# Three-bank rings in PSUM, one TensorE semaphore per step, and a step's other matmuls in front of its sums, in a graph network kernel

## The chip, the core and the metric

The kernel runs on one core of a Trainium2 chip. The metric is device time in microseconds. Before, it was 2964.37 us (median of 3 runs, 2962.93 to 2966.32). The core's engines are TensorE (PE; its weight loads are shown as PEld), VectorE (DVE), ScalarE (ACT), GpSimd (POOL) and SyncE (SP). Each works through a queue of its own in order, and they wait for each other by semaphores.

## The reference

100,000 edges in order of their target run between 6250 nodes of 256 features; each edge has 32 attributes and one of three types. Three layers of

```python
ew = edge_attr @ edge_w + edge_b                 # the same in every layer
inv_cnt[i] = 1 / max(segment_sum(mask_i, dst), 1)
for l in range(3):
    msg = relu(x[src] * ew)
    out = sum_i (segment_sum(msg * mask_i, dst) * inv_cnt[i]) @ weights[l, i]
    out = out + x @ roots[l] + biases[l]
    x = x + relu(out)
return layernorm(x_in + x)
```

## The kernel before

**Tiles and steps.** The edges are 782 tiles of 128; a step q has two tiles, a layer NP = 391 steps. For each tile GpSimd gathers 128 rows of x from HBM (`gather`, L700: an indirect DMA of 128 KB into the ring `xg`, XR = 12 tiles). TensorE makes the edge weights of both tiles in PSUM (`edge_weights`, L867: turned attributes `at` against two parts of `edge_w`). DVE multiplies (L1300), ACT applies the ReLU (L791), TensorE sums by target and type against the 0/1 selectors `S` (`collect`, L911, 4 matmuls of 96 columns, each recorded in two parts), and DVE adds the 96-column result to `acc` in SBUF (`add_sums`, L1138). `S` is made by DVE every other step from a row of numbers kept in PSUM bank 5 (`selectors`, L1097).

**Blocks.** The nodes are NB = 49 blocks of 128, finished in the order `blocks` from step `starts[k]` on (14, 22, 34 ... 374, 393). For each: x is loaded and turned (`turn_x`, L936, bank 4, copied by ACT, L799), four products with the layer's matrices (`mix`, L961, one step each, banks 6 and 7), and DVE's five operations (`block_ops`, L1155 to L1194). SP stores the new rows to the next x and, shifted by one block, to a copy y, from which the next layer's first 12 gathers read while the last block is unfinished.

**Layer 0 alone** also turns the attributes: SP loads four tiles' attributes (`load_attr`), ACT rounds a copy (`high`, L745), DVE subtracts it (`split`, L1012, 128x128), TensorE transposes the four tiles into bank 4 (`attr_turn`, L846), and ACT copies them into `at` (`attr_copy`, L753); SP keeps `at` in HBM (`keep_attr`) and loads it again in layers 1 and 2. It also counts edges by target and type: two matmuls a step (L903), an addition (`add_counts`, L1251), and a matmul per block (`count`, L924).

**Order.** Every engine's queue is written out by hand, step by step. TensorE in iteration q: `edge_weights(q+1)`, `count`, `collect(q-1)`, `mix`, `attr_turn`, `turn_x`. DVE: product q, `add_sums(q-2, 0)`, `selectors`, `split`, block operations, counts, `add_sums(q-2, 1)`. PSUM banks 0 and 1 hold edge weights in turn, 2 and 3 the sums. TensorE has semaphores for the edge weights (`s_e`), each tile's sums (`s_sc`), transposes (`s_tr`, `s_xt`), counts (`s_cm`) and pairs of block products (`s_d0`, `s_d1`). A gather waits until the sums have read its ring slot: `eng.wait_ge(s_sc, 2 * ((n - XR) // 2 + 1))`.

Of the kernel before, what the change touches and what calls it, by code (L numbers as in the profile page):

```python
# [62 lines left out]
def gnn_program(nc, x_in, src, dst, edge_attr, edge_type, weights, roots, biases, edge_w, edge_b,  # L63
                src_t, dst_t, typ_t, head, head7, head4, due, out):
# [7 lines left out]
    NT = 782  # L72
# [10 lines left out]
    XR, SR, TR, AR = 12, 8, 3, 6  # L83
    XB, XT, TB = 4, 2, 4
    PAD = 1000000
    BR = 196
# [29 lines left out]
    with ctx:  # L116
# [18 lines left out]
        hs = sb("hs", [128, 3, 4, 64])  # L135
# [8 lines left out]
        cnt = sb("cnt", [128, 148])  # L144
        diff = sb("diff", [128, 128])
        brow = sb("brow", [128, BR], I32)
# [43 lines left out]
        def columns(k):  # L190
# [20 lines left out]
        s_an = sems("s_an", 3)  # L211
        s_hi, s_lo, s_tr, s_atc = sem("s_hi"), sem("s_lo"), sem("s_tr"), sem("s_atc")
# [3 lines left out]
            "s_oh", "s_ob", "s_cn", "s_cm", "s_inv", "s_df"))  # L216
        s_w = sem("s_w")
        s_xl = sems("s_xl", XB)
        s_x0 = sems("s_x0", 2)
        s_xt, s_xc, s_d0, s_d1, s_f0, s_f1, s_nm, s_z = (sem(n) for n in (  # L220
            "s_xt", "s_xc", "s_d0", "s_d1", "s_f0", "s_f1", "s_nm", "s_z"))
# [4 lines left out]
        s_dm, s_d2, s_hz = sem("s_dm"), sem("s_d2"), sem("s_hz")  # L226
# [22 lines left out]
        short = order.index(quad(NT - 1))  # L249

        def attrs(g):

            return 16 * (g // 3 + 1) + (16 if g % 3 == short % 3 and g >= short else 0)

# [19 lines left out]
        def products(k, m):  # L274

            b = pD[m // 2] if k < NB - 1 else (pT, pT, pD[0], pD[1])[m]
            return b[0:rows(k), 256 * (m % 2):256 * (m % 2) + 256]

        def sums_bank(l, q, i):

            V = l * NP + q
            return pA[(V + (i if q == NP - 1 else 0)) % 2]
# [5 lines left out]
        def twice(K, i):  # L288

            return sum(n % NB < NB - 1 for n in range(i, min(K, NB * (L - 1)), TB))  # L290

# [19 lines left out]
        end = starts[-1] + 16  # L311
# [20 lines left out]
        G_an = hs[:, 0, 0, 0:32]  # L332
# [139 lines left out]
        def general(eng, name):  # L472
# [31 lines left out]
            if name == "sync":  # L504
                eng.wait_ge(s_z0, 2)
                eng.wait_ge(s_src, 32)
                eng.wait_ge(s_pc, 9)
                eng.wait_ge(s_atc, 1)
                for i in range(XR):
                    eng.wait_ge(s_g[i], 16)  # L510
                for g in range(3):
                    eng.wait_ge(s_an[g], attrs(g))
# [31 lines left out]
        def _(eng):  # L544
# [10 lines left out]
            def load_attr(g):  # L555
                if g >= 3:
                    eng.wait_ge(s_tr, g - 2)
                a, n = 128 * head_tile(order[g]), tiles_of(g) - (g == short)
                if g == short:
                    eng.wait_ge(s_hz, 1)  # L560
                    eng.dma_start(hs[0:LAST, g % 3, 3, 32:64], edge_attr[128 * (NT - 1):E, :]).then_inc(s_an[g % 3], 16)
                eng.dma_start(hs[:, g % 3, 0:n, 32:64], edge_attr[a:a + 128 * n, :]
                              .rearrange("(j p) d -> p j d", p=128)).then_inc(s_an[g % 3], 16)

            def keep_attr(g):
                w = 128 * tiles_of(g)
                eng.wait_ge(s_atc, g + 1)
                eng.dma_start(attr_t[g, :, 0:w], at[0:64, g % TR, 0:w].bitcast(F32)).then_inc(s_ao[g % TR], 16)

            def reload_attr(l, g):  # L570
                G = l * NG + g
                eng.wait_ge(s_e, l * NP + 2 * max(0, g - TR + 1))
# [32 lines left out]
            load_attr(2)  # L605
            eng.dma_start(idx[:, 0:2], src_t[:, 0:2]).then_inc(s_src, 16)

            def load_sources(l):
                for k in hosts_k:
                    eng.wait_ge(s_d1, NB * l + k + 1)  # L610
# [6 lines left out]
            def fast():  # L617
                for l in range(L):
                    late = (13, 9, 15)[l]
                    for q in range(-4, end):  # L620
                        if l == 0 and q % 2 == 0:
                            if 3 <= q // 2 + 4 < NG:
# [33 lines left out]
                        for k in starting(q, 8 if l else 12):  # L656
                            if k + XB < NB:
                                load_x(l, k + XB)
                        for k in starting(q, 9):
# [11 lines left out]
        def _(eng):  # L671
            eng.memset(p_ew, 0.0).then_inc(s_ez, 1)
            eng.memset(zcol[:, :], 0.0).then_inc(s_zc, 1)
            eng.memset(hs[:, short % 3, 3, 32:64], 0.0).then_inc(s_hz, 1)
# [52 lines left out]
        def _(eng):  # L727
# [14 lines left out]
            def high(g):  # L742

                eng.wait_ge(s_an[g % 3], attrs(g))
                eng.activation(hs[:, g % 3, :, 0:32].bitcast(F32R), hs[:, g % 3, :, 32:64], ACT.Copy).then_inc(s_hi, 1)  # L745

            def attr_copy(g):
                w = 128 * tiles_of(g)
                eng.wait_ge(s_tr, g + 1)
                if g >= TR:  # L750
                    eng.wait_ge(s_e, 2 * (g - TR + 1))
                    eng.wait_ge(s_ao[g % TR], 16 * (g // TR))
                eng.activation(at[0:64, g % TR, 0:w], pT[0:64, 0:w], ACT.Copy).then_inc(s_atc, 1)  # L753
# [3 lines left out]
            attr_copy(0)  # L757
# [19 lines left out]
            def fast():  # L777
                for l in range(L):
                    for q in range(-6, end):
# [12 lines left out]
                        if l == 0 and q % 2 == 0 and 1 <= (q + 2) // 2 < NG:  # L792
                            attr_copy((q + 2) // 2)
                        for k in [k for k in range(NB) if q == turn_step(k) + 1]:
                            K, n = NB * l + k, rows(k)
                            eng.wait_ge(s_xt, K + 1)
                            if K >= XT:
                                eng.wait_ge(s_d0, K - XT + 1)
# [598 lines left out]
```

## Time and profile before

| | |
|---|---|
| median of 3 runs | 2964.37 us |
| the profiled execution's own span | 3581.6 us |
| busy PE / PEld | 2843.8 us (79%) / 2613.2 us (73%) |
| busy DVE | 2148.4 us (60%) |
| busy ACT | 1289.4 us (36%) |
| busy POOL | 2224.3 us (62%) |
| granted TensorE clock, mean | 0.896 |
| chain that ended last | PE 59%, issue 17%, DVE 9% |
| moved by DMA | 465.42 MB in 334989 packets |

Busy times are of the one recorded execution; shares are of its span. Matmuls are pipelined and their ends are modelled, so TensorE's busy time is not its rate: the distance from start to start in a dense stretch is. "issue" and "remote" as releasers mean that the profile shows nothing, or nothing on this core's engines, that ended the wait.

### The profile page before, as it was taken

Reading aid. Unit: us, or ns where it says so; the run is one execution under the profiler, and the core shown is the slowest. Engines: PE = TensorE matmul, PEld = TensorE weight load, DVE = VectorE, ACT = ScalarE, POOL = GpSimd, SP = SyncE. Lnnn points to the kernel's source line nnn. Section 1 sums busy time; section 2 is a strip of 40 time slices with the busy share of each in tenths; the row PEclk is TensorE's granted clock in tenths of the full one; section 3 lists DMA queues with packets and bytes.
Section 4 is the critical chain, followed back from the end, with each engine's and each line's share of the span. In section 5 each row is a group of like instructions: output and inputs, shape, how many; then the busy total and the mean of one; then the engine's idle time right before and its main releaser. Section 6 shows DMA issues by size and latency. Waiting matters only on the chain.

```text
span 3581.6 us, 59909 instructions
## 1 busy us (share of the span) xinstructions
PE 2843.8 (79%) x18436; PEld 2613.2 (73%) x18436; DVE 2148.4 (60%) x6028; ACT 1289.4 (36%) x2738; POOL 2224.3 (62%) x2364
## 2 busy tenths in 40 slices
PE   6888888888888877787777877777777777787777
PEld 6777777777777777777777777767777777776776
DVE  5666666666666555555555555555556656665665
ACT  5555555555555322222222222222222222222222
POOL 6666666666666566666666666656666666666664
PEclk9999999999999888888898889988888888899898
DMA  6554555555455444444444444444444444444443
GB/s 148 135 137 132 137 135 138 136 137 137 131 137 145 133 120 127 125 130 127 126 127 127 134 124 127 131 127 132 126 124 128 125 127 131 125 130 124 128 128 99
DMA packets 334989, 465.42 MB, mean 130 GB/s; under 512 B 158995, under 2 KB 221646, under 8 KB 334670
## 3 DMA queue, kind: packets, MB, share of 16 engines
q0 software_dynamic: 112608, 307.65, 30.1%
q1 hardware_dynamic: 221244, 153.70, 15.6%
q8 instruction: 156, 2.56, 0.3%
q14 instruction: 163, 1.34, 0.1%
q10 hardware_dynamic: 818, 0.18, 0.0%
HBM read 403.94 MB, written 57.36 MB: 129 GB/s over the span
## 4 chain that ended last, share of the span: by engine, by line
PE 59%; issue 17%; DVE 9%; another core or an unknown queue 8%; ACT 4%; DVEq 2%; DMA 0%; ACTq 0%
PE bank L911 29%; PE bank L867 14%; PE bank L961 12%; DVE acc L1138 4%; PE bank L846 2%; DVE xg L1300 1%; ACT oh_a L812 1%; DVE t L1155 1%; ACT at L753 1%; DVEq L1274 1%; PE bank L936 1%; DVEq L1138 1%; ACT xg L791 1%; DVE S L1097 1%
## 5 line engine op out<-in xcount | busy, mean ns | idle before, releaser
L700 POOL DMA_INDIRECT xg<-x,idx x1540 | 1457.0, 946 | 870.6 <-issue 351.7
L911 PE MATMUL bank<-S,xg 128*128 128x96 f32 x9384 | 1450.5, 304 | 360.3 <-issue 176.3
L911 PEld LDWEIGHTS bank<-S,xg 128*128 128x128 f32 x9384 | 1313.6, 216 | 429.2 <-issue 385.4
L791 ACT ACTIVATE xg<-xg 128x512 f32<-128x512 f32 x1170 | 736.7, 630 | 2102.3 <-DVE xg L1300 1193.8
L1300 DVE TENSOR_TENSOR xg<-xg,bank 128x512 f32<-128x512 f32 x1170 | 800.8, 684 | 691.0 <-remote 329.4
L1138 DVE TENSOR_TENSOR acc<-acc,bank 128x192 f32 x2346 | 816.7, 348 | 570.0 <-PE bank L911 343.0
L867 PE MATMUL bank<-wsb,at 128*128 128x256 f32 x4692 | 985.7, 337 | 213.6 <-issue 123.3
L700 POOL DMA_INDIRECT xg<-in_x_dram,idx x782 | 742.2, 949 | 454.2 <-PE bank L911 211.2
L867 PEld LDWEIGHTS bank<-wsb,at 128*128 128x128 f32 x4692 | 749.3, 214 | 297.6 <-issue 195.9
L961 PE MATMUL bank<-W,acc 128*128 128x256 f32 (+1 forms) x1764 | 515.9, 415 | 7.2 <-issue 6.4
L961 PEld LDWEIGHTS bank<-W,acc 128*128 128x128 f32 (+1 forms) x1764 | 386.9, 258 | 17.3 <-issue 12.1
L1097 DVE TENSOR_TENSOR S<-bank,kr 128x384 f32<-128x384 f32 x588 | 323.2, 550 | 0.8 <-issue 0.7
L812 ACT ACTIVATE oh_a<-iota,lo 128x128 bf16<-128x128 bf16 x782 | 266.2, 389 | 3.5 <-PE bank L911 3.4
L1155 DVE SCALAR_TENSOR_TENSOR t<-bank,inv,t 128x256 f32<-128x256 f32 (+1 forms) x441 | 209.2, 474 | 17.6 <-remote 10.1
L961 PE MATMUL bank<-W,xT 128*128 128x256 f32 (+1 forms) x588 | 200.2, 472 | 0.9 <-issue 0.8
L846 PE MATMUL bank<-ident,hs 128*64 128x128 f32 x782 | 131.3, 295 | 32.5 <-issue 19.2
L961 PEld LDWEIGHTS bank<-W,xT 128*128 128x128 f32 (+1 forms) x588 | 127.9, 238 | 17.3 <-issue 3.0
L903 PE MATMUL bank<-oh_b,oh_a 128*128 128x12 bf16 x782 | 81.2, 175 | 68.2 <-issue 62.5
L753 ACT ACTIVATE at<-bank 64x512 fp32r<-64x512 f32 x196 | 113.3, 578 | 44.1 <-remote 25.8
L1251 DVE TENSOR_TENSOR cnt<-cnt,bank 128x12 f32<-128x12 f32 x391 | 60.7, 155 | 104.7 <-remote 97.0
L903 PEld LDWEIGHTS bank<-oh_b,oh_a 128*128 128x128 bf16 x782 | 52.6, 107 | 95.5 <-issue 75.3
L846 PEld LDWEIGHTS bank<-ident,hs 128*64 128x64 f32 x782 | 93.2, 128 | 39.4 <-issue 35.1
(75 smaller groups left out, 789.7 us busy)
## 6 DMA issues: line engine op xcount, KB each, us to landing
at<-attr_t SPq DMA_DIRECT2D x390, 128.0 KB
attr_t<-at SPq DMA_DIRECT2D x195, 128.0 KB
xg<-x,idx POOLq DMA_INDIRECT x1540
xg<-in_x_dram,idx POOLq DMA_INDIRECT x782
hs<-in_edge_attr_dram SPq DMA_DIRECT2D x194, 64.0 KB
x<-t SPq DMA_DIRECT2D x96, 128.0 KB
xblk<-x SPq DMA_DIRECT2D x96, 128.0 KB
y<-t SPq DMA_DIRECT2D x94, 128.0 KB
```

What stands on the lines that cost most here:

```text
L700: eng.indirect_dma_start(out=xg[:, n % XR, :], out_offset=None, in_=rows_in, in_offset=bass.IndirectOffsetOnAxis(ap=rows_at, axis=0)).then ...
L753: eng.activation(at[0:64, g % TR, 0:w], pT[0:64, 0:w], ACT.Copy).then_inc(s_atc, 1)
L791: eng.activation(v, v, ACT.Relu).then_inc(s_r, 1)
L812: eng.activation(oh_a[:, j % AR, :], iota[:, 1:129], ACT.Sign, bias=lo[:, tile(j):tile(j) + 1]).then_inc(s_oh, 1)
L846: last = eng.transpose(pT[0:64, 128 * i:128 * i + 128], hs[:, g % 3, i, :], ident[:, :])
L867: last = eng.matmul(pE[Q % 2][:, 256 * i:256 * i + 256], at[:, sl, c:c + 128], wsb[:, p, :], start=(p == 0), stop=(p == 1))
L911: last = eng.matmul(sums_bank(l, q, i)[:, 192 * i + 96 * h:192 * i + 96 * h + 96], xg[:, n % XR, 128 * h:128 * h + 128], S[:, slot(l, 2 * ...
L961: last = eng.matmul(o, a, W[:, 2 * (r % 4) + h, :], start=(h == 0), stop=(h == 1))
L1097: eng.tensor_tensor(S[:, at4:at4 + w, :], steps_of[:, 1:WK + 1].unsqueeze(1).to_broadcast([128, w, WK]), kr[:, c:c + w].unsqueeze(2).to_br ...
L1138: eng.tensor_tensor(a, a, sums_bank(l, q, i)[:, 192 * i:192 * i + 192] .rearrange("p (h w) -> p h w", h=2), ALU.add).then_inc(s_acc, 1)
L1155: return eng.scalar_tensor_tensor(tt, products(k, m), inv[0:n, 3 * blocks[k] + r:3 * blocks[k] + r + 1], tt, ALU.mult, ALU.add)
L1300: eng.tensor_tensor(v, v, pE[Q % 2][:, :].rearrange("p (i d) -> p i d", i=2), ALU.mult).then_inc(s_m, 1)
```

## The change

- **Rings.** Edge weights, turned x and the last block's first product share three banks (0, 1, 4) in the order of their use (`shared_bank`); the sums go to three banks (2, 3, 5). Edge weights are made two steps ahead, and the sums are added three steps later (`add_sums(q-3)`).
- **Semaphores.** TensorE announces a step once, by its last sum (`s_sc`). Edge weights (from step 3 of a layer), turned rows, counts and block products have no semaphore of their own: who needs them waits for the next sums in the queue (`wait_edges`, `turned`, `mixed`).
- **Order.** In TensorE's iteration the block products and `turn_x` stand in front of `collect`.
- **Attributes.** The host hands them over turned, twice (`attr_2`, 64 rows). ACT copies both halves into `at` with rounding (`high`), DVE subtracts in the second half (`split`, now 32x512). `attr_turn` and `attr_copy` are gone, and the ring `hs` has two slots.
- **Small things.** The selectors' row of numbers stands in each of the three banks of the sums (97 columns, copied three times at the start); `oh_b` subtracts its offset itself; `keep_counts` copies a block's counts (49 copies of 128x3) before its count matmul; the table of bases `brow` is 64x392 in place of 128x196; stores and loads on SP and the zeroing on ACT move by one or two steps.

The diff, cut to its core:

```diff
-    BR = 196
+    HR2 = 2
+    BR = 392
-        hs = sb("hs", [128, 3, 4, 64])
+        hs = sb("hs", [128, HR2, 512])
+        kept = sb("kept", [128, 2, R])
-        pE = bank[0:2]
-        pA = bank[2:4]
-        steps_of = bank[5][:, 0:148]
+        pE = [bank[0], bank[1], bank[4]]
+        pA = [bank[2], bank[3], bank[5]]
-            return starts[k] - (2 if k < NB - 1 else 7)
+            return starts[k] - (3 if k < NB - 1 else 7)
-            return starts[k] + (2 * m if wide(l, k) else 1 + m)
+            return starts[k] + 1 + m + (m // 2 if wide(l, k) else 0)
+        def collected(l, q):
+            return l * (NP + 1) + q + 1 + (q == NP - 1)
+        def mixed(l, k, m):
+            return collected(l, mix_step(l, k, m) - 1)
+        def turned(l, k):
+            return collected(l, turn_step(k) - 1)
+        def wait_edges(eng, l, q):
+            if q < 3:
+                eng.wait_ge(s_e, 3 * l + q + 1)
+            else:
+                eng.wait_ge(s_sc, collected(l, q - 3))
+        def sums_bank(l, q, i):
+            V = l * NP + q
+            return pA[(V + (i if q == NP - 1 else 0)) % 3]
+        def steps_of(l, q, a, b):
+            return pA[(l * NP + q) % 3][:, 384 + a:384 + b]
+        def shared_bank(what, l, i):
+            return pE[turn_of[what, l, i] % 3]
...
 (SP)
             def load_attr(g):
-                if g >= 3:
-                    eng.wait_ge(s_tr, g - 2)
+                if g >= HR2:
+                    eng.wait_ge(s_lo, g - HR2 + 1)
+                a, w = 128 * head_tile(order[g]), 128 * tiles_of(g)
+                eng.dma_start(hs[0:64, g % HR2, 0:w], attr_2[:, a:a + w]).then_inc(s_an[g % HR2], 16)
             def keep_attr(g):
-                eng.wait_ge(s_atc, g + 1)
+                eng.wait_ge(s_lo, g + 1)
-                    late = (13, 9, 15)[l]
+                    late = (11, 10, 16)[l]
-                            if 0 <= q // 2 < NG:
-                                keep_attr(q // 2)
+                            if 0 <= q // 2 + 2 < NG:
+                                keep_attr(q // 2 + 2)
...
 (GpSimd)
                 if n >= XR:
-                    eng.wait_ge(s_sc, 2 * ((n - XR) // 2 + 1))
+                    eng.wait_ge(s_sc, collected(*divmod((n - XR) // 2, NP)))
...
 (ACT)
             def high(g):
-                eng.activation(hs[:, g % 3, :, 0:32].bitcast(F32R), hs[:, g % 3, :, 32:64], ACT.Copy).then_inc(s_hi, 1)
-            def attr_copy(g):
-                eng.wait_ge(s_tr, g + 1)
-                eng.activation(at[0:64, g % TR, 0:w], pT[0:64, 0:w], ACT.Copy).then_inc(s_atc, 1)
+                eng.activation(at[0:64, g % TR, 0:w], hs[0:64, g % HR2, 0:w], ACT.Copy).then_inc(s_hi, 1)
...
 (TensorE)
-            def attr_turn(g):
-                for i in range(tiles_of(g)):
-                    last = eng.transpose(pT[0:64, 128 * i:128 * i + 128], hs[:, g % 3, i, :], ident[:, :])
-                last.then_inc(s_tr, 1)
             def edge_weights(l, q):
-                last.then_inc(s_e, 1)
+                if q < 3:
+                    last.then_inc(s_e, 1)
             def collect(l, q):
-                elif V >= 2:
-                    eng.wait_ge(s_acc, 2 * (V - 1))
+                elif V >= 3:
+                    eng.wait_ge(s_acc, 2 * (V - 2))
-                    last.then_inc(s_sc, 1)
+                    if i or q == NP - 1:
+                        last.then_inc(s_sc, 1)
             def fast():
                 for l in range(L):
                     for q in range(-3, end):
-                        if (1 if l else 0) <= q < NP - 1:
-                            edge_weights(l, q + 1)
+                        if (0 if l else -1) <= q < NP - 2:
+                            edge_weights(l, q + 2)
...
+                        for k in range(NB):
+                            for m in range(R + 1):
+                                if q == mix_step(l, k, m):
+                                    mix(l, k, m)
+                        for k in range(NB):
+                            if q == turn_step(k):
+                                turn_x(l, k)
                         if 0 <= q - 1 < NP:
                             collect(l, q - 1)
-                        for k in range(NB):
-                            for m in range(R + 1):
-                                if q == mix_step(l, k, m):
-                                    mix(l, k, m)
-                        if l == 0 and q % 2 and 1 <= (q + 3) // 2 < NG:
-                            attr_turn((q + 3) // 2)
-                        for k in range(NB):
-                            if q == turn_step(k):
-                                turn_x(l, k)
...
 (DVE)
             def split(g):
-                raw, high = hs[:, g % 3, :, 32:64], hs[:, g % 3, :, 0:32]
-                eng.tensor_tensor(raw, raw, high, ALU.subtract).then_inc(s_lo, 1)
+                eng.tensor_tensor(at[32:64, g % TR, 0:w], hs[32:64, g % HR2, 0:w],
+                                  at[32:64, g % TR, 0:w].bitcast(F32), ALU.subtract).then_inc(s_lo, 1)
-            link(eng.tensor_copy(steps_of, iota[:, :]))
+            for q in range(3):
+                link(eng.tensor_copy(steps_of(0, q, 0, WK + 1), iota[:, 0:WK + 1]))
+            def keep_counts(k):
+                eng.tensor_copy(kept[:, k % 2, :], cnt[:, 3 * blocks[k]:3 * blocks[k] + 3]).then_inc(s_cs, 1)
-                        if 0 <= q - 2 < NP:
-                            add_sums(l, q - 2, 0)
+                        if 0 <= q - 3 < NP:
+                            add_sums(l, q - 3, 0)
-                        if l == 0 and q % 2 and 1 <= (q + 6) // 2 < NG:
-                            split((q + 6) // 2)
+                        if l == 0 and q % 2 == 0 and 1 <= (q + 4) // 2 < NG:
+                            split((q + 4) // 2)
-                            if q == starts[k] + 2 and k < NB - 1:
+                            if q == starts[k] + 3 and k < NB - 1:
                                 todo[k] = block_ops(l, k)
...
 (host)
+    attr_2 = _np.zeros((2, 32, 128 * 782), _np.float32)
+    attr_2[:, :, 0:100000] = _np.ascontiguousarray(inputs["edge_attr_32"]).T
```

## Rows read from the trace of the kernel before

**Rows 1.** The head of the page.

```profile
span 3581.6 us, 59909 instructions
```

**Rows 2.** Groups of instructions by line; busy us, mean ns, idle before.

```profile
L700 POOL DMA_INDIRECT xg<-x,idx x1540 | 1457.0, 946 | 870.6 <-issue 351.7 <-PE bank L911 291.8 <-remote 227.2
...
L700 POOL DMA_INDIRECT xg<-in_x_dram,idx x782 | 742.2, 949 | 454.2 <-PE bank L911 211.2 <-issue 169.8 <-remote 71.9
...
L700 POOL DMA_INDIRECT xg<-y,idx x24 | 22.7, 945 | 11.8 <-issue 5.5 <-remote 3.8 <-PE bank L911 2.5
```

**Rows 3.** Timeline of POOL, layer 1; start us, us, what, idle before.

```profile
1905.64 0.94 POOL L700 DMA_INDIRECT xg<-x,idx  x1 [1.78 <-PE bank L911]
...
1911.90 0.96 POOL L700 DMA_INDIRECT xg<-x,idx  x1 [0.30 <-issue]
1914.60 0.94 POOL L700 DMA_INDIRECT xg<-x,idx  x1 [1.74 <-remote]
```

**Rows 4.** Windows: length, busy (xcount) PE, PEld, DVE, ACT, POOL; clock, DMA share, GB/s.

```profile
701.78:707.91 6.13, 5.24 (x46) 4.90 (x44) 3.54 (x13) 2.81 (x8) 3.78 (x4) 1.00 0.45 119
1905.64:1914.60 8.96, 7.24 (x52) 7.00 (x50) 4.82 (x13) 1.26 (x2) 5.69 (x6) 1.00 0.36 105
```

**Rows 5.** Timeline of POOL: the first and the last gather.

```profile
4.73 1.10 POOL L700 DMA_INDIRECT xg<-in_x_dram,idx  x1 [0.97 <-DMA idx<-in_src_t_dram]
...
3561.22 0.95 POOL L700 DMA_INDIRECT xg<-x,idx  x1 [0.30 <-issue]
```

**Rows 6.** Timeline of PE, layer 0, at full clock.

```profile
706.63 0.60 PE L846 MATMUL bank<-ident,hs 128*64 128x128 f32 x4 [0.89 <-ACT xT L799]
706.98 0.72 PE L867 MATMUL bank<-wsb,at 128*128 128x256 f32 x4
707.54 0.21 PE L903 MATMUL bank<-oh_b,oh_a 128*128 128x12 bf16 x2
707.60 1.11 PE L911 MATMUL bank<-S,xg 128*128 128x96 f32 x8
708.55 1.11 PE L961 MATMUL bank<-W,acc 128*128 128x256 f32 x4
```

**Rows 7.** Timeline of PE, layer 1, at full clock.

```profile
1908.13 1.12 PE L961 MATMUL bank<-W,acc 128*128 128x256 f32 x4
1908.90 0.83 PE L867 MATMUL bank<-wsb,at 128*128 128x256 f32 x4
1909.56 1.03 PE L911 MATMUL bank<-S,xg 128*128 128x96 f32 x8
```

**Rows 8.** Timeline of DVE, layer 0: two steps.

```profile
714.70 0.69 DVE L1300 TENSOR_TENSOR xg<-xg,bank 128x512 f32<-128x512 f32 x1 [0.38 <-issue]
...
717.42 0.28 DVE L1012 TENSOR_TENSOR hs<-hs 128x128 f32<-128x128 f32 x1
717.62 0.48 DVE L1155 SCALAR_TENSOR_TENSOR t<-bank,inv,t 128x256 f32<-128x256 f32 x1
...
718.75 0.68 DVE L1300 TENSOR_TENSOR xg<-xg,bank 128x512 f32<-128x512 f32 x1
```

**Rows 9.** Timeline of all engines: DVE operations with two SBUF inputs, and gathers.

```profile
8.11 0.97 DVE L1026 TENSOR_TENSOR acc<-acc 128x782 f32<-128x782 int32 x1
...
8.66 1.24 POOL L700 DMA_INDIRECT xg<-in_x_dram,idx  x1 [0.30 <-issue]
...
710.30 0.29 DVE L1012 TENSOR_TENSOR hs<-hs 128x128 f32<-128x128 f32 x1
710.41 0.99 POOL L700 DMA_INDIRECT xg<-in_x_dram,idx  x1 [0.30 <-issue]
```

**Rows 10.** Timeline of all engines, end of layer 0.

```profile
1211.74 0.75 DVE L1290 TENSOR_TENSOR xg<-xg,bank 128x256 f32<-128x256 f32 x2
...
1228.27 0.94 POOL L700 DMA_INDIRECT xg<-x,idx  x1 [10.02 <-PE bank L911]
```

**Rows 11.** Groups of instructions by line, of the split.

```profile
L1012 DVE TENSOR_TENSOR hs<-hs 128x128 f32<-128x128 f32 x196 | 55.7, 285 | 4.4 <-ACT hs L745 3.4 <-issue 1.1
```

More of the change, by code:

```diff
@@ L290, in twice, with free_shared_bank, products @@
             return sum(n % NB < NB - 1 for n in range(i, min(K, NB * (L - 1)), TB))
+        end = starts[-1] + 18
+        users = [("edges", 0, 0)]
+        for l in range(L):
+            for q in range(-3, end):
+                if (0 if l else -1) <= q < NP - 2:
+                    users.append(("edges", l, q + 2))
+                if l < L - 1 and q == NP + 1:
+                    users.append(("edges", l + 1, 0))
+                if l < L - 1 and q == end - 1:
+                    users.append(("edges", l + 1, 1))
+                if q == mix_step(l, NB - 1, 0):
+                    users.append(("last", l, NB - 1))
+                users += [("turned", l, k) for k in range(NB) if q == turn_step(k)]
+        turn_of = {u: i for i, u in enumerate(users)}
+        def shared_bank(what, l, i):
+            return pE[turn_of[what, l, i] % 3]
+        def free_shared_bank(eng, what, l, i):
+            before = turn_of[what, l, i] - 3
+            if before < 0:
+                return
+            what, l, i = users[before]
+            if what == "edges":
+                eng.wait_ge(s_m, l * NP + i + 1)
+            elif what == "turned":
+                eng.wait_ge(s_xc, NB * l + i + 1)
+            else:
+                eng.wait_ge(s_f0, NB * l + i + 1)
+        def products(l, k, m):
+            last = shared_bank("last", l, NB - 1)
+            b = pD[m // 2] if k < NB - 1 else (last, last, pD[0], pD[1])[m]
+            return b[0:rows(k), 256 * (m % 2):256 * (m % 2) + 256]
         hosts = [16, 12]
@@ L507, in general @@
                 eng.wait_ge(s_pc, 9)
-                eng.wait_ge(s_atc, 1)
+                eng.wait_ge(s_lo, 1)
                 for i in range(XR):
                     eng.wait_ge(s_g[i], 16)
-                for g in range(3):
-                    eng.wait_ge(s_an[g], attrs(g))
+                for g in range(HR2):
+                    eng.wait_ge(s_an[g], 16)
             phase(start_steps())
@@ L1166, in first @@
                         eng.wait_ge(s_yo[i], 16 * twice(K, i))
-                    op(eng.tensor_tensor(tt, products(k, 0), bias[0:n, :], ALU.add))
+                    op(eng.tensor_tensor(tt, products(l, k, 0), bias[0:n, :], ALU.add))
                 def mean0():
@@ L1240, in block_ops @@
                 if wide(l, k):
-                    return [o for f in ops for o in (f, pause)]
+                    return [first, mean0, pause, mean1, mean2, residual]
                 return ops if l < L - 1 else ops + [add_x, stats, aggr, pause, recip, shift]
@@ L1247, in add_counts @@
                 if q == NP - 1:
-                    eng.wait_ge(s_sc, NT)
+                    eng.wait_ge(s_sc, collected(0, q))
                 eng.wait_ge(s_cn, q)
-                eng.wait_ge(s_cm, sum(p - 1 <= q for p in starts))
-                eng.tensor_tensor(cnt[:, f:f + HW], cnt[:, f:f + HW], pA[q % 2][:, 384:384 + HW],
-                                  ALU.add).then_inc(s_cn, 1)
+                eng.tensor_tensor(cnt[:, f:f + HW], cnt[:, f:f + HW], counts_at(q), ALU.add).then_inc(s_cn, 1)
+            def keep_counts(k):
+                eng.wait_ge(s_cn, min(NP, starts[k] - 2))
+                if k >= 2:
+                    eng.wait_ge(s_sc, collected(0, starts[k - 2]))
+                eng.tensor_copy(kept[:, k % 2, :], cnt[:, 3 * blocks[k]:3 * blocks[k] + 3]).then_inc(s_cs, 1)
             def count_ops(k, i):
```

208 lines of the change are left out of this document (102 added, 106 removed).

## The prediction

> **What bounds the kernel now.** I read the profile in four steps.
>
> First the page's head against the times: the profiled execution spans 3581.6 us [rows 1], the median of the runs is 2964.37. The recorded run is 617 us longer, so its idle time can't be taken at its word; what the recorder adds has to be found first.
>
> Second, the groups of instructions, by count times duration for each engine. One group stands out: GpSimd's gathers, 1540 + 782 + 24 = 2346 of them for 1457.0 + 742.2 + 22.7 = 2221.9 us busy [rows 2]. TensorE has more busy time in all, but spread over modelled, overlapping matmuls.
>
> Third, the timeline of GpSimd in the middle of a layer. A gather takes 0.94 to 0.96 us and 0.30 us pass before the next, whatever is waited for: from 1905.64 to 1911.90 five gathers start, one each 1.25 us [rows 3]. Then comes a hole, 1.74 us in place of 0.30. Such holes (gathers over 2 us behind the one before; there are 470, the one of [rows 3] among them) stand six gathers apart in layers 1 and 2 and four apart in layer 0, and in them DVE, ACT and TensorE stand still too. In time that is 6.13 us against 8.96, in counted instructions 115 against 123 [rows 4]; over the trace it is 59909 instructions [rows 1] / 470 = 127 for each hole. A stall that comes by the number of recorded instructions and stops every engine is the recorder's.
>
> Fourth, without these holes: 4.7 us to the first gather [rows 5], 2345 x 1.25 = 2931 us, and 3581.6 - 3561.2 = 20.4 us from the last gather's start to the end [rows 1, 5]. Sum 2956 us, 8 us (0.3%) under the median of the runs. What 2346 gathers cost in sequence on GpSimd's queue is thus the kernel's time, within 0.3%. The gather's ring of 12 tiles lets GpSimd run six steps ahead, and a step (two tiles) is 2.50 us of it.
>
> Do the other engines fit under 2.50? TensorE, at full clock, in layer 0: four attribute transposes every other step 706.98 - 706.63 = 0.35, edge weights 0.56, counts 0.06, sums 0.95 [rows 6], a block product 0.77 [rows 7]. With 4 x 49 block products over 391 steps: 0.35/2 + 0.56 + 0.06 + 0.95 + 0.50 x 0.77 = 2.13 us a step. In layer 1: edge weights 0.66, the same sums and products, 0.66 + 0.95 + 0.39 = 2.00 us [rows 6, 7]. DVE in layer 0: two steps in 718.75 - 714.70 = 4.05 us [rows 8], that is 2.03 each. All are below 2.50. Layer 0 on TensorE is the nearest, at 85%.
>
> **The change part by part.**
>
> *Attributes turned on the host.* It removes 782 PE transposes: 196 x 0.35 = 69 us of TensorE's queue in layer 0 [rows 6], its step falls to 1.95. It also takes the 196 copies out of bank 4 and one chain (ACT, DVE, PE, ACT) down to ACT, DVE. GpSimd's queue hides all of this: 2.13 was already under 2.50. Worth 0. If that cover were gone (gathers shorter without the recorder), it would be worth up to 69 us.
>
> *The split on DVE* goes from 128x128 elements (285 ns, [rows 11]) to 32x512. Its nearest row is the product of 512 elements a partition, 0.69 us [rows 8]. It starts the next instruction 0.60 later, the old split 0.20 later (717.42 to 717.62). So +0.40 per two steps, and the 49 new copies of counts and the count's new place add at most 0.16: 4.05 + 0.56 = 4.6 us of 5.0. Hidden, with 8% to spare. Queued behind it on DVE are a block operation and the second sum's addition, which TensorE needs only three steps later.
>
> *Its effect on GpSimd.* A gather that starts inside a DVE operation with two SBUF inputs is longer: the split at 710.30 ran to 710.59, the gather of 710.41 took 0.99; p_dst minus p_head ran 8.11 to 9.08, the gather of 8.66 took 1.24 [rows 9]. Both are the operation's end plus 0.82 us. So GpSimd waits once, some 0.13 us after its start. The new split can hold it up to 0.69 - 0.13 = 0.55 us, the old one up to 0.15. Bounds: gain 2 us (the old hits, 52 of 196 by about 0.04 us, are gone) to loss 196 x 0.55 = 108 us. A hit needs the split to start in some 0.55 us of the 1.25 us of a gather; by chance 42%, by 0.27 us, 22 us in all. But DVE in this regime follows the landing of gathers, so its phase is fixed and the hit comes always or never. I take never (0), and keep 22 as a rival.
>
> The Trainium skill (SBUF — State Buffer, "SBUF: two separate sides") says that GpSimd and a DVE operation with two SBUF inputs share a port pair, and that whichever starts first keeps it for the whole instruction. What it would do here is rival D. The trace agrees with the first half; a split that started after its gather has no long gather beside it, and in reverse none shows a wait of DVE that could be told apart.
>
> *Semaphores.* One per step on TensorE in place of one per matmul group. Products and edge weights are now announced by the step's sums, so DVE hears of them later by what stands between: at most sums and counts, about 1 us. The product's three-bank rings give a whole step (2.5 us) for it. GpSimd's own wait is the same event, the last sum of the step six back. Nothing on its queue is added or removed. Bounds: 0 to a loss of 1 us once per layer end; I take 0.
>
> *Edge weights two steps ahead, block products, turned rows and counts in front of the sums.* On TensorE's queue at most 0.66 + 0.77 us now stand before a step's sums [rows 7], so the ring's release to GpSimd is later by that. The ring holds 15 us, from which a gather, its landing, product, ReLU and sums are paid; the slack is several us. Worth 0 in the steady state. SP's stores and loads move past queue waits for the split instead of the copy, by two steps; each is needed four or more steps later.
>
> *Ends.* Start: three 97-column copies and a larger first row of bases cost DVE some 0.6 us, one transposition chain less gives about 1 us back. Layer ends: in the recorded run, last product to first gather of the new x takes 1228.27 - 1211.74 = 16.5 us [rows 10], with a hole and slow matmuls in it. GpSimd has 12 gathers = 15 us to issue from the shifted copy meanwhile; added waits of 1 us vanish or cost 1 us. Tail: 0 to +1. Together -1 to +3, taken as -1.
>
> Sum: 2964.4 + 0 - 1 = **2963 us**.
>
> **The rivals.**
>
> *A, gathers set the time in both (0.50):* 2963, own range 2958.5 to 2970.
>
> *B, the 8 us that the sum leaves are losses of before (0.15).* In layer 0 TensorE is at 85% of GpSimd's pace at full clock, and block-rich stretches exceed it; DVE's two-input operations may hit gathers. The new order takes both away: 2964 - 8 = 2956. For it: a step with two block products comes to 0.56 + 0.06 + 0.95 + 2 x 0.77 = 3.1 us there [rows 6, 7]. Against it: six steps of ring absorb that.
>
> *C, the change gains what it says (0.13).* If an unrecorded gather is shorter than 1.25, then TensorE or the loop between PE, DVE and ACT is the bound, and 69 us of transposes and half a waiting time go: about 2964 - 69 - 15 = 2880. Against it speaks the agreement to 0.3%, which would be chance.
>
> *D, slower by the port (0.15):* each split of layer 0 delays a gather. It decides as soon as the split starts within 0.55 us ahead of a gather: 2963 + 22 = 2985, and at worst 3071.
>
> *E, slower by DVE in layer 0 (0.07):* if its two steps exceed 5.0 us because waits are added to its 4.6 us: 0.15 us x 196 = 30, so 2993.
>
> **How the numbers follow.** The measurement can tell about 0.2%, that is 6 us. Same is A, 0.50. Faster is B and C, 0.28. Slower is D and E, 0.22. The range of 8 in 10 leaves out C and the upper parts of D and E: 2945 to 2990.
>
> **What would show it right or wrong.** Right: 2346 gathers still 1.25 us apart between holes, 0.94 to 0.96 long also in layer 0; holes fewer by the recorded instructions that went, so the profiled span falls by tens of us while the unrecorded time doesn't move; TensorE's busy time lower by about 70 us or more. D shows as gathers of 1.1 to 1.5 us in layer 0 beside the split's line; E as idle GpSimd in layer 0 released by sums. C is shown wrong by an unchanged time, and right by a time under 2940: then the step that fails is the first, that a gather costs 1.25 us also when nothing is recorded.

## The result, and the profile after

The changed kernel takes 2997.03 us (median of 4 runs, 2993.55 to 2999.45) against 2964.33 for the kernel before (4 runs, 2962.93 to 2966.32): a ratio of 1.0107 [1.0092, 1.0121], **slower by 33 us**. The forecast was 2963, its range 2945 to 2990: the result lies above it. Two executions of runs further down lie far out (5815.84 us, one of a_pr's eleven; 7979.54, one of a_rs4's six); the ratios leave them out.

The head of the page and its busy times, after:

```profile
span 2991.8 us, 57658 instructions
...
PE 2552.9 (85%) x17654; PEld 2388.0 (80%) x17654; DVE 2262.5 (76%) x6079; ACT 1247.2 (42%) x2542; POOL 2245.3 (75%) x2363
```

The recorded execution is as long as the others, where that of before was 617 us longer [rows 1]. It has none of the holes of [rows 3, 4]. So after can't be laid beside the recorded execution of before; the kernel before was recorded again (b_again, below), this time without holes too. Against it TensorE's busy time fell by 62 us (2615.0 to 2552.9), near the forecast 70 or more, and DVE's rose by 122 (2140.7 to 2262.5).

Groups of instructions by line, after (busy us, mean ns of one | idle before, releasers), which answer to [rows 2] and [rows 11]:

```profile
L756 POOL DMA_INDIRECT xg<-x,idx x1540 | 1460.4, 948 | 476.0 <-issue 403.5 <-PE bank L955 72.6
L756 POOL DMA_INDIRECT xg<-in_x_dram,idx x782 | 759.8, 972 | 243.0 <-issue 202.3 <-PE bank L955 39.5 <-DMA idx<-in_src_t_dram 1.2
L1046 DVE TENSOR_TENSOR at<-hs,at 32x512 fp32r<-32x512 f32 x196 | 133.9, 683 | 12.3 <-ACT at L805 6.2
L756 POOL DMA_INDIRECT xg<-y,idx x24 | 22.7, 946 | 7.3 <-issue 6.4 <-PE bank L955 0.9
```

The 1540 gathers of layers 1 and 2 take 948 ns, those from y 946. Only layer 0's 782 take 972. They are the ones beside which the new split runs (196 times 683 ns, in place of 285). Against the 946 to 950 ns of the others that is 22 to 26 ns x 782, 17 to 20 us.

The timeline of GpSimd and of the split shows how, in layer 0 (start us, us, what, idle before):

```profile
205.21 0.68 DVE L1046 TENSOR_TENSOR at<-hs,at 32x512 fp32r<-32x512 f32 x1
205.50 1.21 POOL L756 DMA_INDIRECT xg<-in_x_dram,idx  x1 [0.30 <-issue]
...
210.78 0.95 POOL L756 DMA_INDIRECT xg<-in_x_dram,idx  x1 [0.31 <-issue]
211.36 0.68 DVE L1046 TENSOR_TENSOR at<-hs,at 32x512 fp32r<-32x512 f32 x1
212.03 0.94 POOL L756 DMA_INDIRECT xg<-in_x_dram,idx  x1 [0.30 <-issue]
...
215.77 0.73 DVE L1046 TENSOR_TENSOR at<-hs,at 32x512 fp32r<-32x512 f32 x1
215.78 0.95 POOL L756 DMA_INDIRECT xg<-in_x_dram,idx  x1 [0.30 <-issue]
...
220.65 0.68 DVE L1046 TENSOR_TENSOR at<-hs,at 32x512 fp32r<-32x512 f32 x1
220.78 1.37 POOL L756 DMA_INDIRECT xg<-in_x_dram,idx  x1 [0.30 <-PE bank L955]
222.46 0.94 POOL L756 DMA_INDIRECT xg<-in_x_dram,idx  x1 [0.30 <-issue]
```

Read each gather against the split ahead of it, by the prediction's formula (the split's end plus 0.82 us). The first: the split ends at 205.89, plus 0.82 is 206.71, less 205.50 is 1.21, the length shown. The last: 221.33 + 0.82 - 220.78 = 1.37. A split 0.67 us ahead of its gather (211.36) lengthens nothing, nor does it hold the gather that began before it (210.78). Four splits in a row lie 0.29, 0.67, 0.01 and 0.13 us ahead of the next gather: **the phase is not fixed**. Counted over layer 0, 70 of 196 splits lengthen a gather, by 0.26 us in the mean, 18 us in all.

The second place is the start of layer 2. Timeline of GpSimd, SP's queue and edge weights, after:

```profile
1998.18 1.60 SPq L638 DMA_DIRECT2D xblk<-x  x4
...
1999.82 0.67 SPq L644 DMA_DIRECT2D lo<-in_x_dram  x2
2000.54 4.55 SPq L632 DMA_DIRECT2D at<-attr_t  x3
...
2007.20 0.95 POOL L756 DMA_INDIRECT xg<-x,idx  x1 [0.30 <-issue]
...
2010.29 1.22 PE L910 MATMUL bank<-wsb,at 128*128 128x256 f32 x4 [4.79 <-DMA at<-attr_t]
2013.44 0.94 POOL L756 DMA_INDIRECT xg<-x,idx  x1 [5.29 <-PE bank L955]
```

The edge weights wait 4.79 us for attributes that SP asked for only behind six loads of x and its residual; GpSimd, whose ring is then full, waits 5.29 us for the sums. TensorE's granted clock is 0.50 from 2007.7 to 2014.6, and the four edge weights take 1.22 us there. b_again has the same place, smaller, at full clock (0.74 us for the four):

```profile
1996.23 0.74 PE L867 MATMUL bank<-wsb,at 128*128 128x256 f32 x4 [3.72 <-DMA at<-attr_t]
...
1998.34 0.95 POOL L700 DMA_INDIRECT xg<-x,idx  x1 [3.00 <-PE bank L911]
```

The third is the end. Timelines of all engines, last gather, last product and last block products, of after and then of b_again:

```profile
2971.93 0.95 POOL L756 DMA_INDIRECT xg<-x,idx  x1 [0.31 <-issue]
...
2976.14 0.74 DVE L1340 TENSOR_TENSOR xg<-xg,bank 128x256 f32<-128x256 f32 x2
...
2980.54 4.53 PE L1000 MATMUL bank<-W,acc 128*128 128x256 f32 x12 [1.69 <-DVE acc L1176]
```

```profile
2954.29 0.95 POOL L700 DMA_INDIRECT xg<-x,idx  x1 [0.30 <-issue]
...
2957.56 0.75 DVE L1290 TENSOR_TENSOR xg<-xg,bank 128x256 f32<-128x256 f32 x2
...
2961.49 2.92 PE L961 MATMUL bank<-W,acc 128*128 128x256 f32 x12 [0.65 <-DVE acc L1138]
```

From the last gather to the last product it is 4.21 us, before 3.27: sums are added three steps late, so more additions stand in DVE's queue ahead of it (six, before four). The twelve last products then take 4.53 in place of 2.92. From the last gather to the end: 2991.8 - 2971.9 = 19.9 against 2971.0 - 2954.3 = 16.7.

The twelve products are the same in both kernels; what differs is **TensorE's granted clock**. Windows around them (length, busy PE, PEld, DVE, ACT, POOL; clock, DMA share, GB/s), after and then b_again:

```profile
2980.50:2985.10 4.60, 4.53 (x12) 3.54 (x12) 0.96 (x2) 0.00 (x0) 0.00 (x0) 0.63 0.03 7
```

```profile
2961.40:2964.40 3.00, 2.91 (x12) 2.58 (x12) 1.00 (x3) 0.00 (x0) 0.00 (x0) 1.00 0.02 5
```

At a clock of 1.00 the twelve products of a layer's last block take 2.90 to 2.93 us wherever they were recorded, in both kernels; at 0.50 they take 5.47 (a_reload2, below). So 1.6 of the 3.2 us by which the end is longer go with the clock. It is lower over the whole run too: the mean is 0.918 to 0.930 in the four runs of the changed kernel and 0.957 to 0.972 in all runs of the kernel before on the two chips without holes. The prediction did not have this. In the middle of a layer the gathers hide it: from layer 1's first gather to layer 2's it is 979.0 us at 0.94 after, and 978.5 at 0.96 in b_longp (below). Why the changed kernel is granted less is not shown.

### The profile page after: what moved, and what is told of

Read it like the earlier page. It is cut to its first block, busy times and chain, and to the rows that moved or that the text cites. A ratio compares the mean times of both kernels' runs of the same rounds, so it can differ in the third digit from the quotient of the medians.

```text
span 2991.8 us, 57658 instructions
## 1 busy us (share of the span) xinstructions
PE 2552.9 (85%) x17654; PEld 2388.0 (80%) x17654; DVE 2262.5 (76%) x6079; ACT 1247.2 (42%) x2542; POOL 2245.3 (75%) x2363
## 4 chain that ended last, share of the span: by engine, by line
PE 32%; POOL 30%; DMA 15%; issue 14%; DVE 8%; DVEq 0%; ACT 0%; ACTq 0%; SPq 0%; POOLq 0%
POOL xg L756 30%; PE bank L955 15%; DMA xg<-x,idx 10%; PE bank L910 9%; PE bank L1000 7%; DMA xg<-in_x_dram,idx 4%; DVE xg L1350 3%; DVE acc L1176 2%; DVE at L1046 1%; PE bank L976 0%; DVE t L1193 0%; DMA at<-attr_t 0%; PE bank L947 0%; DVE cnt L1288 0%; DVE t L1205 0%
## 5 line engine op out<-in xcount | busy, mean ns | idle before, releaser
L756 POOL DMA_INDIRECT xg<-x,idx x1540 | 1460.4, 948 | 476.0 <-issue 403.5
L955 PE MATMUL bank<-S,xg 128*128 128x96 f32 x9384 | 1345.2, 290 | 22.1 <-DVE acc L1176 15.7
L955 PEld LDWEIGHTS bank<-S,xg 128*128 128x128 f32 x9384 | 1269.6, 206 | 48.4 <-ACT xg L842 21.0
L910 PE MATMUL bank<-wsb,at 128*128 128x256 f32 x4692 | 912.9, 320 | 234.6 <-DVE xg L1350 214.9
L756 POOL DMA_INDIRECT xg<-in_x_dram,idx x782 | 759.8, 972 | 243.0 <-issue 202.3
L910 PEld LDWEIGHTS bank<-wsb,at 128*128 128x128 f32 x4692 | 690.0, 206 | 286.3 <-issue 182.4
L864 ACT ACTIVATE oh_a<-iota,lo 128x128 bf16<-128x128 bf16 x782 | 266.1, 387 | 15.7 <-PE bank L955 14.8
L976 PE MATMUL bank<-ident,xblk 128*128 128x128 f32 (+1 forms) x294 | 62.3, 295 | 133.8 <-DVE xg L1350 132.9
L976 PEld LDWEIGHTS bank<-ident,xblk 128*128 128x128 f32 (+1 forms) x294 | 31.7, 145 | 163.2 <-issue 161.9
L1000 PE MATMUL bank<-W,xT 128*128 128x256 f32 (+1 forms) x588 | 156.8, 389 | 0.0
L1046 DVE TENSOR_TENSOR at<-hs,at 32x512 fp32r<-32x512 f32 x196 | 133.9, 683 | 12.3 <-ACT at L805 6.2
L805 ACT ACTIVATE at<-hs 64x512 fp32r<-64x512 f32 x196 | 120.1, 613 | 6.2 <-DMA hs<-in_attr_dram 4.1
L1000 PEld LDWEIGHTS bank<-W,xT 128*128 128x128 f32 (+1 forms) x588 | 101.9, 192 | 8.0
```

The source lines that it names most:

```text
L756: eng.indirect_dma_start(out=xg[:, n % XR, :], out_offset=None, in_=rows_in, in_offset=bass.IndirectOffsetOnAxis(ap=rows_at, axis=0)).then ...
L864: eng.activation(oh_a[:, j % AR, :], iota[:, 1:129], ACT.Sign, bias=lo[:, tile(j):tile(j) + 1]).then_inc(s_oh, 1)
L910: last = eng.matmul(shared_bank("edges", l, q)[:, 256 * i:256 * i + 256], at[:, sl, c:c + 128], wsb[:, p, :], start=(p == 0), stop=(p == 1))
L955: last = eng.matmul(sums_bank(l, q, i)[:, 192 * i + 96 * h:192 * i + 96 * h + 96], xg[:, n % XR, 128 * h:128 * h + 128], S[:, slot(l, 2 * ...
L1000: last = eng.matmul(o, a, W[:, 2 * (r % 4) + h, :], start=(h == 0), stop=(h == 1))
L1046: eng.tensor_tensor(at[32:64, g % TR, 0:w], hs[32:64, g % HR2, 0:w], at[32:64, g % TR, 0:w].bitcast(F32), ALU.subtract).then_inc(s_lo, 1)
```

## The experiments

Time is compared with runs of the kernel before on the same chip; two chips gave 2964.9 to 2967.2 for it, a third 3538 (last part of this section).

**b_again** is the kernel before, once more.

> The kernel before, unchanged, timed and profiled once more. It measures what two equal programs differ by (within 0.2%, 2958 to 2970), and it may be recorded without the holes. Theory P (GpSimd's 2346 gathers set the time): if the record is clean, its span is near 2962, gathers start 1.25 us apart in all layers, and the lengthened gathers of layer 0 sum to under 5 us (the kernel after: 20.7). Theory Q (DVE or TensorE set layer 0's time before): gathers of layer 0 wait for sums in the middle of the layer.

2965.46 us, ratio 0.9997 [0.9988, 1.0007]; its recorded span is 2971.0, at the upper edge of its runs. There are no holes, and the pitch of gathers is 1.25 us. Its layer 0, by line:

```profile
L700 POOL DMA_INDIRECT xg<-in_x_dram,idx x782 | 745.0, 953 | 239.4 <-issue 168.6 <-PE bank L911 70.6 <-DVE flag L1057 0.3
```

So the sum of the prediction's fourth view stands (a gather each 1.25 us sets the time), and the base for layer 0 is 953 ns, not 972: 14.8 us less than after.

**a_psum** is the changed kernel with the split's second operand read from PSUM, from the fifth group of attributes on. It subtracts a number in place of the rounded attributes, so the exact low part is left out.

```diff
-                eng.tensor_tensor(at[32:64, g % TR, 0:w], hs[32:64, g % HR2, 0:w],
-                                  at[32:64, g % TR, 0:w].bitcast(F32), ALU.subtract).then_inc(s_lo, 1)
+                less = (steps_of(0, 2 * g - 4, 1, 2)[32:64, :].to_broadcast([32, w]) if g >= 4
+                        else at[32:64, g % TR, 0:w].bitcast(F32))
+                eng.tensor_tensor(at[32:64, g % TR, 0:w], hs[32:64, g % HR2, 0:w], less, ALU.subtract).then_inc(s_lo, 1)
```

> The kernel after with the split's second input read from PSUM (a constant zero there) instead of SBUF, from the fifth group on: as long on DVE, but one SBUF input. What is left out is the subtraction, so the low part of the attributes is wrong. Theory P: the 18 us of gathers lengthened by the split go, 2979 (2975 to 2983). Theory Q (the split costs by DVE's time): no change, 2997 (2993 to 3001).

2978.42 us, 1.0041 [1.0027, 1.0055]. Run a second time beside the changed kernel (a_again) on another chip:

> The kernel after, unchanged, once more, as the base for the three runs beside it. The runs so far fell on two chips: on one the kernel before takes 2964 to 2966 us, on the other 3538, with the holes of the first trace in the record. On the first chip 2997 (2994 to 3000) is expected, on the other one 3538 + 22 = 3560 (3553 to 3568), since there GpSimd's queue has slack in its holes and part of the lengthened gathers vanishes.

> As a_psum (the split's second input from PSUM, the subtraction left out), beside the kernel after on the same chip. Theory P: 18 us under a_again on a chip without holes, less on one with them. Theory Q: level with a_again.

a_again 2994.40 (4 runs, 1.0094 [1.0078, 1.0109]), a_psum2 2977.30 (1.0037 [1.0023, 1.0051]): 17 us less by the place of one operand. The groups by line of a_psum2, and behind them two lines of the timeline of a_psum:

```profile
L756 POOL DMA_INDIRECT xg<-in_x_dram,idx x782 | 742.0, 949 | 241.9 <-issue 198.6 <-PE bank L955 42.5 <-DMA idx<-in_src_t_dram 0.8
...
L1048 DVE TENSOR_TENSOR at<-hs,bank 32x512 fp32r<-32x512 f32 x192 | 130.4, 679 | 6.0
```

```profile
309.07 0.68 DVE L1048 TENSOR_TENSOR at<-hs,bank 32x512 fp32r<-32x512 f32 x1
309.23 0.95 POOL L756 DMA_INDIRECT xg<-in_x_dram,idx  x1 [0.30 <-issue]
```

679 ns a split, yet the gathers are back at 949, and one that starts 0.16 us into a split takes 0.95. DVE's time is not the cause; its two SBUF inputs are.

**b_long and b_longp** put the cause into the kernel before: one more operation on DVE after each split, its result unused, with both inputs in SBUF or one in PSUM.

```diff
+                    eng.tensor_tensor(bank[5][32:64, 152:512].rearrange("p (a b) -> p a b", a=3),
+                                      ident[32:64, 0:120].unsqueeze(1).to_broadcast([32, 3, 120]),
+                                      ident[32:64, 0:120].unsqueeze(1).to_broadcast([32, 3, 120]), ALU.subtract).then_inc(s_dum, 1)
```

(Cut to its core: the first group is left out, and each such operation waits for the one before. b_longp: the third line reads `steps_of` in PSUM.)

> The kernel before with a second DVE operation of 32x360 elements with two SBUF inputs after each of 195 splits, its result unused. It takes about 0.53 us and can hold a gather for 0.53 - 0.13 = 0.40 us; by chance 0.38/1.25 = 30% of them do, by 0.2 us: 12 us. Theory P: 2964 + 12 = 2976 (2970 to 2984). Theory Q: DVE's queue alone, two steps 4.05 + 0.45 = 4.5 of 5.0 us, hidden: 2964; or a loss of the same size as in b_longp.

> As b_long, but the added operation reads one of its inputs from PSUM. Same DVE time, no second SBUF input. Theory P: no change to before, 2964 (2960 to 2968). Theory Q: the same loss as b_long.

2974.31 (1.0031 [1.0020, 1.0042]) and 2966.77 (1.0006 [0.9997, 1.0015]). Both operations are about equally long (537 and 533 ns); only the one with two SBUF inputs costs, 7.5 us more. Layer 0's gathers, b_long first:

```profile
L701 POOL DMA_INDIRECT xg<-in_x_dram,idx x782 | 750.4, 960 | 241.2 <-issue 169.1 <-PE bank L912 71.0 <-DMA idx<-in_src_t_dram 0.8
```

```profile
L701 POOL DMA_INDIRECT xg<-in_x_dram,idx x782 | 742.9, 950 | 240.3 <-issue 161.7 <-PE bank L912 78.3 <-DVE flag L1064 0.3
```

742.9 to 750.4 is the same 7.5 us. 104 us more work on DVE in layer 0 (b_longp) cost nothing that can be told from noise (1.2 us), so rival E is not what happens at this pace.

**a_reload2 and a_rs4b.** The first is the changed kernel with the fetch of the attributes that layers 1 and 2 miss put ahead of the loads of x; the second also makes four operations of 128 columns of each split.

```diff
-                        if l and q % 2 == 0 and TR <= q // 2 + 2 < NG:
+                        if l and q % 2 == 0 and TR < q // 2 + 2 < NG:
                             reload_attr(l, q // 2 + 2)
...
                         if q == 0:
+                            if l:
+                                reload_attr(l, TR)
                             for i in range(TB if l else 0):
```

```diff
...
+                for c in range(0, w, 128):
+                    ins = eng.tensor_tensor(at[32:64, g % TR, c:c + 128], hs[32:64, g % HR2, c:c + 128],
+                                            at[32:64, g % TR, c:c + 128].bitcast(F32), ALU.subtract)
+                ins.then_inc(s_lo, 1)
```

> As a_reload (the fourth group of attributes loaded again before the loads of x), now beside the kernel after on the same chip. Theory P: 5 us under a_again. Rival: level with it (within 2 us).

> As a_rs4 (a_reload, and the split in four pieces of 128 columns), beside the kernel after on the same chip. Theory P (lengthened gathers cost): 16 us under a_again and 11 under a_reload2 on a chip without holes, less on one with them. Theory Q (DVE's time costs): level with a_reload2 or slower.

a_reload2 took 2991.01 (1.0082 [1.0068, 1.0096]), 3.4 us under a_again, less than the expected 5, and the two intervals overlap. In layer 2 the wait of 5.17 us (a_again) fell to 1.66. But in the same record layer 1 has a wait of 5.34 where a_again has 1.47, behind twelve block products that take 5.47 us at a clock of 0.50 (2.90 in a_again, at 1.00):

```profile
1015.94 5.47 PE L1002 MATMUL bank<-W,acc 128*128 128x256 f32 x12
...
1027.85 0.94 POOL L758 DMA_INDIRECT xg<-x,idx  x1 [5.34 <-PE bank L957]
...
2007.05 0.94 POOL L758 DMA_INDIRECT xg<-x,idx  x1 [1.66 <-PE bank L957]
```

From the last gather to the end it has 17.1 us, with the products at full clock, where a_again has 18.6. So the cause of layer 2's wait is shown, by its going; what it is worth in time is not clear of noise.

a_rs4b took 2977.08 (1.0034 [1.0022, 1.0046]), another 14 us less:

```profile
L758 POOL DMA_INDIRECT xg<-in_x_dram,idx x782 | 746.6, 955 | 245.6 <-issue 203.8 <-PE bank L957 41.0 <-DMA idx<-in_src_t_dram 0.8
...
L1050 DVE TENSOR_TENSOR at<-hs,at 32x128 fp32r<-32x128 f32 x782 | 174.9, 278 | 11.8 <-ACT at L807 4.8 <-issue 1.0
```

DVE spends 41 us more on the split than with one operation (174.9 against 133.9), and the kernel is faster: a gather waits only for the short operation that it meets, 0.28 us and not 0.68. 63 of 782 lengthen a gather, by 4.7 us in all.

**a_pr** joins the PSUM operand and the earlier fetch.

> a_psum and a_reload in one: the split's second input from PSUM (the subtraction left out) and the fourth group of attributes loaded again earlier. Theory P, additive: 17 + 3 us under the kernel after, 2974 (2971 to 2977), so 8 us stay over the kernel before for a later start, a longer end and layer 2's lengthened gathers. Rival: some other cost of the new order is larger, 2980 or more.

2970.22, 1.0019 [1.0009, 1.0028]. With both causes gone about 5 us are left over the kernel before (3 to 8 by the interval).

**b_skip2 and a_skip2** leave out every fourth gather, from a layer's 13th on, in both kernels (the tiles then use the rows that stand in the ring), so that GpSimd no longer sets the pace.

```diff
+        def left_out(n):
+            return n % 4 == 3 and n % NT >= 2 * AHEAD
...
+                if left_out(n):
+                    return
                 eng.indirect_dma_start(
```

> As b_skip: every fourth gather left out, sums wrong. On a chip without holes TensorE's dense rows give 2397 us and the waits come on top: 2430 to 2550. If TensorE's order were what bound the kernel before, it would stay over 2900.

> As a_skip, beside b_skip2. Theory that the new order itself costs nothing and pays where gathers give way: 20 to 100 us under b_skip2 (a_skip was 29 us under b_skip on the chip with holes). Rival (the order costs, the gathers' slack hid a part of it): level with b_skip2 or over it.

2460.06 (0.8299 [0.8286, 0.8311]) and 2484.39 (0.8376 [0.8363, 0.8389]). A quarter fewer gathers takes 17% off the kernel before: it was bound by them. Behind them stands TensorE. But the changed kernel, whose transposes of 69 us (as the prediction priced them) are gone, is 24 us **slower** there too. In the two records the loss is in layer 0, which is 39 us longer (922.1 us from the start to layer 1's first gather, against 883.2); the rest is 11 us shorter. Busy times of layer 0 (window; PE, PEld, DVE, ACT, POOL; clock, DMA share, GB/s), b_skip2 and then a_skip2:

```profile
100.00:700.00 600.00, 599.62 (x4982) 581.22 (x4982) 523.08 (x1720) 470.92 (x1175) 379.65 (x402) 1.00 0.60 156
```

```profile
100.00:700.00 600.00, 559.33 (x4273) 521.25 (x4272) 573.13 (x1688) 431.98 (x1003) 378.79 (x387) 0.97 0.58 164
```

TensorE is busy in all of the window before; after, DVE is the busiest, to 96%, and TensorE to 93%. The 69 us of TensorE that rival C hoped for are thus not there even when GpSimd sets the pace no more. In their place stand, by these shares, DVE's 78 us more for splits (133.9 - 55.7, [rows 11]): rival E's mechanism at a pace that the real kernel doesn't reach. No run takes the split's time away at this pace, so that much is read and not tested.

**The third chip** ran four kernels, the same as a_reload2, a_rs4b, b_skip2 and a_skip2:

> The kernel after with one transfer moved on SP's queue: at the start of layers 1 and 2 the fourth group of attributes is loaded again before the loads of x, not after them. In the trace of after TensorE waits 4.79 us for it at 2010 us and GpSimd then 5.3 us for TensorE. Theory P (gathers set the time, each of their waits counts): 5 us less than after, 2992 (2988 to 2995), and no gather start later than 3 us behind the one before in layer 2. Rival (the wait only moves to another transfer): no change, 2997.

> As a_reload, and the split done as four DVE operations of 128 columns instead of one of 512. More DVE time (4 x 0.20 against 0.60 in two steps), but one can hold a gather for at most 0.29 - 0.13 = 0.16 us: 4 x 195 x 0.13/1.25 x 0.08 = 6.5 us in place of 18. Theory P: 2997 - 5 - 11 = 2981 (2976 to 2986). Theory Q (DVE's time in layer 0 costs): slower than a_reload, 2997 or more.

> The kernel before with every fourth gather left out (from the 13th of a layer on); the tile's old contents are used in its place, so the sums are wrong. GpSimd's queue is then 2346 x 0.75 x 1.25 = 2210 us and no longer the longest. It asks what sets the time behind it. By the dense rows: TensorE 2.13 us a step in layer 0 and 2.00 in layers 1 and 2, 2397 us, and the waits between PE, DVE and ACT on top: 2430 to 2550. If gathers did not set the time before, it is within 1% of 2964.

> The kernel after with every fourth gather left out in the same way. Theory that the change does what it says once gathers give way: TensorE's step in layer 0 is 1.95 and the loops are looser, so 50 us or more under b_skip. Rival: DVE's two steps of layer 0 (4.6 us and more) set layer 0, so it is level with b_skip or over it by up to 60 us.

The kernel before took 3538.09 us there (11 runs, 3535.61 to 3542.18), a_reload 3555.50 (1.0050 [1.0037, 1.0063]), a_rs4 3556.81 (1.0050 [1.0037, 1.0063]), b_skip 2909.20 (0.8228 [0.8216, 0.8240]), a_skip 2879.98 (0.8139 [0.8127, 0.8150]). The records have the holes of [rows 3, 4], and the timed runs have the length that goes with them. The expectations were worked out for the other chips, and their times missed. The fetch and the split can't be priced from these four, since stalls of some 1.5 us every 130 or so instructions hide effects of 0.2 us. That is why they were repeated above. Even the sign of the skipped pair is the other there: the changed kernel has fewer instructions, and so, if the holes go by them, fewer holes (not counted).

## Why the prediction was wrong

**What bounds the kernel: right.** 2346 gathers 1.25 us apart set the time; b_again shows it without holes, b_skip2 by taking gathers away, and the sum of 2956 lies 0.3% under the median as before. **Holes: right to leave out, wrong in their cause as put.** They go with one chip of three; timed runs there have the length that goes with them. Whether recording has a part in them stays open.

**The split's effect on GpSimd: the step that failed.** The formula (the operation's end plus 0.82 us), the window of 0.55 us, and what a hit by chance would cost (42% of splits, 0.27 us, 22 us) came out nearly as worked out: 36%, 0.26 us, 18 us. Wrong was the choice of 0: "its phase is fixed and the hit comes always or never". DVE follows landings only in its product. The split stands behind additions, selectors and block operations that change from step to step, and four splits in a row already lie at four phases. Two steps of [rows 8] were too few to call a phase fixed, and without that reason the expected value should have stood in the sum. Priced by removal: 17 us (a_psum2 under a_again), 14 with four short operations (a_rs4b under a_reload2). With the expected value of 22 in the sum, the forecast would have been 2985; the rest of the miss is in the ends.

**Attributes turned on the host: 0, right** at this pace, and with the split that it needs worth nothing in layer 0 behind it either (a_skip2). **DVE's load: right**: 104 us more hid (b_longp).

**Semaphores and two steps ahead: 0 in the steady state, right (layer 1: 979.0 us against 978.5); at the ends mis-sized, the second step that failed.** The sum had -1, bounds -1 to +3. Against b_longp, whose recorded execution is of 2962.7 us, after's is 29.1 longer. By the groups of lines: layer 0's gathers 759.8 - 742.9 = 16.9, the others 0.6, GpSimd's idle time (476.0 + 243.0 + 7.3) - (470.2 + 240.3 + 7.3) = 8.5, from last gather to end 19.9 - 16.7 = 3.2. So some 12 us are waits, mostly in three places: layer 2's start (5.29 us, against 3.00 in b_again and 1.18 in b_longp), the first wait for a ring slot (2.76 us; 0.98 in b_again, 2.13 in b_longp), and the end, half of it by the granted clock. I had put every moved load four or more steps ahead of its reader. That doesn't hold for the edge weights, which now ask one step sooner for attributes that SP fetches behind six other loads. Only this place was tested by a run of its own (a_reload2), and its price is not clear of noise. The start and the end were seen and not tested; a_pr leaves 5 us for them. And all estimates of TensorE were made at full clock: that the changed kernel would be granted less was no term of the sum, and its cause stays open.

**The rivals.** D was right in kind and in size (its 22 against 18; a share of the splits, though, and not each), and fell short of the result by the ends: 2964 + 17 + 12 = 2993, measured 2997. A is refuted by a_psum2 against a_again: gathers set the time, but not with the same length. B would have the kernel 8 us under before once the port's cost is gone; a_pr is 5 over. C is refuted by b_again (gathers 1.25 us apart without holes) and, for the worth of the transposes, by a_skip2; E for this pace by b_longp.

**The rule on the shared port.** The Trainium skill (SBUF — State Buffer, "SBUF: two separate sides") says that whichever starts first keeps the port for its whole instruction. Its first half is what costs here: the split that is under way holds the gather to its end. The second half is not what the trace shows: a split that starts more than some 0.05 us after a gather is not held, though that gather runs on (the split at 211.36 begins 0.58 us into the gather of 210.78, and takes 0.68). By the rule the 152 of 196 splits that begin while a gather runs would have to wait for it; all but a few take their 0.68 us. The same page ("Who interferes with whom") has that a DVE operation with at most one SBUF input, outside its two-port modes, doesn't contend with GpSimd: b_longp and a_psum2 agree (gathers of 950 and 949 ns).

## What to carry to other kernels

When GpSimd's queue of indirect DMAs sets the time, count the DVE operations with two SBUF inputs, and price each by chance: its length less 0.13 us, over the pitch, is the share that meets a gather, and half of that length is what a hit costs, unless a trace shows the same phase many times over. This estimate goes by the square, so long operations cost most; the runs gave 18 us for 196 of 0.68 us (the estimate: 24), 7.5 for 195 of 0.54 (13), and 4.7 for 782 of 0.28 (7). Reading one operand from PSUM cost no DVE time here (679 ns against 683), and cutting the operation into four was worth more than the 41 us of DVE that it cost. And when a consumer is moved a step ahead, follow each of its inputs to its place in the queue that issues it, at the start of every layer as well as in the middle. And look at the granted clock beside each stretch before a longer one is put down to the order of the work.

## What was new of the hardware

- **The wait goes the other way too, but short.** The nine splits of after that start 0.00 to 0.04 us ahead of a gather take 0.72 to 0.76 us in place of 0.68, and their gathers 0.95 (215.77, above). From about 0.04 us ahead, the gather waits instead (up to 1.46 us).
- **The same program took 2965 to 2967 us on two chips and 3538 on a third**, with stalls of all engines every 130 or so recorded instructions (in a_reload 428 gathers start over 2 us behind the one before, in 57658 instructions). A comparison of times across chips would have been worthless, and the ratio of two kernels changed as well (the skipped pair).
